# Routing slots computed per token, finer vector pieces between the score maxima, and a rearranged GpSimd queue in a one-core attention and tree feed-forward kernel

## The chip, the cores and the metric

The kernel runs on one core of a Trainium2 chip. The metric is device time in microseconds (us) for one launch. The engines are PE (TensorE: matmuls, transposes and, shown apart as PEld, weight loads), DVE (VectorE), ACT (ScalarE), POOL (GpSimd) and SP (SyncE, which here only issues DMAs). Each has its own instruction queue, worked in order, and waits on semaphores.

## What is computed

The input is 4 batches of 750 tokens with 128 features. In order:

```python
y = conv(sign(x), sign(kernel), taps=3)            # 4 x 748 x 64
h = (y + bias - moving_mean) * rsqrt(moving_var + 1e-3) + beta
qkv = layernorm(h) @ Wqkv + bqkv                   # 8 heads of 64
score = q . k * 64 ** -0.5 ; attn = softmax(score, axis=1)
av = attn[n, n] * v[n]                             # only the diagonal is used
h = h + av.reshape(b, n, 512) @ W0 + b0
x2 = layernorm(h) ; node = 0
for level in range(8):                             # a binary tree of 255 nodes
    score = x2 . w1s[node] + b1s[node]
    out += gelu(|score|) * (x2 @ w2s[node] + b2s[node])
    node = 2 * node + 1 + (score > 0)
h = h + out
```

## The kernel before

**Opening.** SP loads x. DVE makes signs, PE transposes them and runs the convolution, DVE turns it into h (`center`: scale, shift, two sums, difference, square) in four groups of six tiles, POOL computes the power -0.5 (`rstd1`), DVE multiplies (`normalise`), ACT and POOL split the result into two fp16 halves (`x_hi`, `x_lo`), and PE transposes it (fill "xh"). Group 0 serves the first projections. Before the loop DVE also centres groups 1 and 2; group 3 follows inside unit 0.

**Loop.** 16 units u (4 batches of 4 head pairs), each of 12 steps i (2 heads, 6 tiles of 125 tokens). A step is one score block of 125x748: PE `scores` (L914, four matmuls), DVE `maxima` (L1354), ACT `exps` (L1183). Three PSUM tiles rotate, so PE may be at most three steps ahead of ACT. The softmax denominator comes from the exps; the diagonal scores come from an elementwise product of q and k (POOL `qk_prod`) summed by PE (fill "d", L797), then `diag_shift` and `diag_weights` on DVE with `diag_exp` on ACT.

**Fills.** A hand-written table, `fills(u, i)`, says which smaller PE job follows the scores of a step: projections of q and k for unit u+2, value times W0 ("yt", or "yp" for the last batch), the convolution and transposes of the remaining groups, and the routing jobs of the batch before. All fills share the two halves of one PSUM tile in turn, and each is taken out of it by ACT one step earlier in ACT's order or by DVE one step later in DVE's. Other work is placed by (u, i) in the loops of DVE and ACT, and by u in POOL's loop. b is u//4 - 1, the batch whose attention is finished, and ph is u % 4. POOL's work per unit is `qk_lo` (low halves and product for unit u+2), `add_heads`, the second layer norm (`ln2_squares`, `ln2_rstd`, `ln2_x`; DVE does its reductions `ln2_sums` and `ln2_sumsq`), and `own_slots`: six indirect DMAs that scatter a batch's token rows into the table `sorted_rows` in HBM.

**Routing.** For batch b: transposes "t", node logits "L", `right_turns`, leaf match "A", `leaf_of_token` (mT: a 0/1 matrix, leaf by token), `leaf_counts` (a running count Ct along the tokens, then small column arithmetic), group prefix "pf", `group_slots`, then `slot_terms`: six DVE operations over 128x750 that turn the rank of each token into its slot, fp32 matmuls "sl" (L899) that sum over leaves, and `slots`. The last two batches' routing follows the last score, in the 4 pseudo-units after unit 15.

**Leaf stage.** SP loads sorted rows, PE multiplies them with the tree's matrices, ACT makes the gates, DVE weighs and sums, POOL scatters the output. It needs all rows scattered, and the low levels' table `wlow`, whose lower half POOL zeroes (L705) after the last score before SP puts the bias rows in.

## Time and profile before

| | us |
|---|---|
| median of 3 runs (563.11 to 563.93) | 563.47 |
| the profiled execution | 557.76 |
| its span | 555.8 |
| PE busy | 385.2 (69%) |
| DVE busy | 377.9 (68%) |
| ACT busy | 287.9 (52%) |
| POOL busy | 280.2 (50%) |

The page names no engine that is busy all the time. Its groups show 192 exps at 862 ns, 192 maxima at 931 ns and 768 score matmuls; before the exps ACT was idle for 95.3 us, nearly all of it released by a maximum, and before the maxima DVE was idle for 44.2 us. A busy share of the whole span therefore says little here: the reader looks at the stages (opening to 46 us, units 0 to 15 to 358.5 us, end of the routing to 424 us, leaf stage to 555.8 us) and within them at which engine was waiting and for whom. The stage table, and the timeline of a few stretches, are the views for that.

### The profile page before, as it was taken

Reading aid. Unit: us, or ns where it says so; the run is one execution under the profiler, and the core shown is the slowest. Engines: PE = TensorE matmul, PEld = TensorE weight load, DVE = VectorE, ACT = ScalarE, POOL = GpSimd, SP = SyncE. Lnnn points to the kernel's source line nnn. Section 1 sums busy time; section 2 is a strip of 40 time slices with the busy share of each in tenths; the row PEclk is TensorE's granted clock in tenths of the full one; section 3 lists DMA queues with packets and bytes.
Section 4 is the critical chain, followed back from the end, with each engine's and each line's share of the span. In section 5 each row is a group of like instructions: output and inputs, shape, how many; then the busy total and the mean of one; then the engine's idle time right before and its main releaser. Section 6 shows DMA issues by size and latency. Waiting matters only on the chain.

```text
span 555.8 us, 8129 instructions
## 1 busy us (share of the span) xinstructions
PE 385.2 (69%) x2554; PEld 261.6 (47%) x2554; DVE 377.9 (68%) x599; ACT 287.9 (52%) x688; POOL 280.2 (50%) x355
## 2 busy tenths in 40 slices
PE   0358589888958887839977788842304988787781
PEld 0245466555535544526644565520303766554450
DVE  1588766888855888997888956479601999842432
ACT  1346687998865876738957535300001333254551
POOL 5253748378894475674886331467181555512211
PEclk9977988999986998968998957555556999999996
DMA  5242423469498331230333000096014111000000
GB/s 121 70 108 60 108 59 84 112 150 199 108 158 141 84 83 27 57 83 19 95 83 84 1 2 0 16 133 70 3 45 128 31 52 49 9 6 7 6 2 6
DMA packets 58423, 36.98 MB, mean 67 GB/s; under 512 B 31645, under 2 KB 57079, under 8 KB 58378
## 3 DMA queue, kind: packets, MB, share of 16 engines
q1 hardware_dynamic: 54250, 33.55, 29.4%
q0 software_dynamic: 3328, 2.36, 1.7%
q10 hardware_dynamic: 800, 0.49, 0.4%
q8 instruction: 26, 0.43, 0.3%
q14 instruction: 19, 0.16, 0.1%
HBM read 11.15 MB, written 7.50 MB: 34 GB/s over the span
## 4 chain that ended last, share of the span: by engine, by line
DVE 34%; PE 27%; ACT 15%; issue 10%; POOL 8%; DMA 3%; DVEq 1%; POOLq 0%; ACTq 0%
PE Z L914 9%; ACT Z L1183 8%; DVE nm L1354 7%; DVE pre L1595 6%; PE Z L1051 4%; DVE va L1587 3%; DMA pre<-in_x 2%; ACT q L1125 2%; PE Z L1053 2%; POOL sorted_rows L649 2%; ACT k L1125 2%; POOL va L617 2%; PE Z L797 2%; DVE pre L320 2%; PE Z L1057 1%
## 5 line engine op out<-in xcount | busy, mean ns | idle before, releaser
L1183 ACT ACTIVATE Z<-Z,nm 125x748 f32<-125x748 f32 x192 | 165.4, 862 | 95.3 <-DVE nm L1354 94.4
L1354 DVE TENSOR_REDUCE nm<-Z 125x1 f32<-125x748 f32 x192 | 174.4, 931 | 44.2 <-PE Z L914 38.1
L914 PE MATMUL Z<-pool_a 128*125 128x512 f16 (+1 forms) x768 | 177.0, 361 | 36.8 <-ACT Z L1183 33.3
L914 PEld LDWEIGHTS Z<-pool_a 128*125 128x125 f16 x768 | 94.9, 150 | 85.8 <-ACT Z L1183 55.8
L721 POOL DMA_INDIRECT out<-pre,va x44 | 42.7, 971 | 87.3 <-DVE pre L1601 78.6
L1595 DVE TENSOR_REDUCE pre<-va 128x64 f32<-128x512 f32 x44 | 45.2, 1027 | 1.3
L1267 ACT COPY va<-Z 32x520 f32<-32x520 f32 x48 | 27.8, 580 | 30.0 <-PE Z L1057 26.6
L649 POOL DMA_INDIRECT sorted_rows<-xrow,slot x24 | 29.1, 1210 | 22.9 <-DVE slot L1488 15.4
L785 PE MATMUL Z<-xhT,wq 128*128 128x249 f16 (+1 forms) x192 | 34.5, 303 | 8.4 <-DVEq L1364 6.7
L1051 PE MATMUL Z<-pool_a,qk 128*32 x96 | 29.6, 390 | 14.2 <-ACT va L1267 8.8
L1183 ACT ACTIVATION_READ_ACCUMULATOR Z<-Z,nm 125x1 f32 x192 | 39.3, 205 | 0.0
L1587 DVE TENSOR_TENSOR va<-Z,gw 128x512 f32<-128x512 f32 x32 | 21.7, 679 | 24.3 <-ACT gw L1248 24.3
L591 POOL CAST pool_a<-q 128x748 f16<-128x748 f32 x14 | 11.3, 806 | 50.7 <-ACT q L1125 49.8
L1587 DVE TENSOR_TENSOR va<-va,gw 128x512 f32<-128x512 f32 x12 | 8.3, 692 | 38.3 <-ACT gw L1248 38.3
L617 POOL TENSOR_TENSOR va<-va 125x256 f32<-125x256 f32 (+2 forms) x54 | 29.6, 548 | 8.4 <-DVE va L1383 5.5
L797 PEld LDWEIGHTS Z<-sel,qk 128*125 128x125 f32 x192 | 28.5, 215 | 5.3 <-issue 1.6
L1239 ACT COPY qk<-Z 65x512 f32<-65x512 f32 x11 | 6.4, 581 | 45.0 <-PE Z L995 44.8
L601 POOL TENSOR_TENSOR qk<-q,k 128x748 f32<-128x748 f32 x16 | 29.4, 1838 | 0.0
L785 PEld LDWEIGHTS Z<-xhT,wq 128*128 128x128 f16 x192 | 19.7, 109 | 19.4 <-DVEq L1364 10.5
L797 PE MATMUL Z<-sel,qk 128*125 128x2 f32 x192 | 27.4, 248 | 0.4 <-DVE pre L1430 0.4
L593 POOL TENSOR_TENSOR pool_a<-q,pool_a 128x748 f16<-128x748 f32 x15 | 24.3, 1617 | 4.0 <-DVE pool_a L1309 2.9
L1016 PE MATMUL Z<-pool_a,qk 128*128 128x260 f32 x64 | 22.4, 433 | 4.4 <-DVE va L1587 4.1
(229 smaller groups left out, 653.8 us busy)
## 6 DMA issues: line engine op xcount, KB each, us to landing
pool_a<-pool_a SPq DMA_DIRECT2D x64, 187.0 KB, 3.3
pool_a<-pool_a SPq DMA_DIRECT2D x64, 93.5 KB, 2.2
sorted_rows<-zrow SPq DMA_DIRECT2D x1, 3640.0 KB, 21.1
va<-sorted_rows SPq DMA_DIRECT2D x11, 260.0 KB, 3.6
w<-in_L_ffn_w2s SPq DMA_DIRECT2D x1, 2048.0 KB, 16.9
pre<-in_x SPq DMA_DIRECT2D x4, 375.0 KB
pool_a<-in_L_ffn_w2s SPq DMA_DIRECT2D x1, 1024.0 KB
out<-pre,va POOLq DMA_INDIRECT x44
```

The lines of the kernel that those rows point to most:

```text
L601: gp.tensor_tensor(qk[:, w % 3, 0:N], q32[:, w % 2, 0:N], k32[:, w % 2, 0:N], ALU.mult).then_inc(s_prod, 1)
L617: link(gp.tensor_tensor(pw[:, 0:n], pw[:, 0:n], pw[:, n:2 * n], ALU.add))
L649: gp.indirect_dma_start(rows, bass.IndirectOffsetOnAxis(slots[0:XP, t:t + 1].bitcast(u32), 0), xrow[0:XP, t, :], None, bounds_check=SLOTS - 1,
L721: gp.indirect_dma_start(outf, bass.IndirectOffsetOnAxis(ids.bitcast(u32), 0), yo[:, k % NO, :], None, bounds_check=T - 1, oob_is_err=False ...
L785: last = mm(z[:, PSUM_AT[c] % 512:PSUM_AT[c] % 512 + CLASS_N[c]], wq[:, a, g * H * D + j * P:g * H * D + (j + 1) * P], xhT[:, r0:r0 + CLAS ...
L797: last = mm(z[0:XP, t:t + NT + 1:NT], qk[:, w % 3, KST[t]:KST[t] + XP], sel[:], start=True, stop=True)
L914: last = mm(z[0:XP, c0:c1], kst[:, u % 3, a, hd, KST[t]:KST[t] + XP], qst[:, u % 3, hd, c0:c1], start=(a == 0), stop=(a == 1))
L1051: mm(y[:, 0:4 * E1], xg, wlow[:, bass.ds(node(g, 4) * (4 * E1) + T03 * E1, 4 * E1)], start=True, stop=True)
L1183: sc_.activation(z, z, ACT.Exp, bias=nm[0:XP, u % 4, i:i + 1], accum_out=sm[0:XP, u % 4, i:i + 1]).then_inc(s_exp, 1)
L1354: v.tensor_reduce(nm[0:XP, u % 4, i:i + 1], Z[n % 3][0:XP, 0:N], X, ALU.max, negate=True).then_inc(s_max, 1)
L1587: v.tensor_tensor(wy[:, k % 2].rearrange("p (h l o) -> p h l o", h=2, o=D), y[:, :, :, 0:D], gw[:, k % 4].rearrange("p (h l) -> p h l", h= ...
L1595: v.tensor_reduce(yo[:, k % NO, :], wy[:, k % 2].rearrange("p (l o) -> p o l", o=D), X, ALU.add).then_inc(s_sl, 1)
```

## The change

- **Opening.** PE computes the batch-norm rows before the first transposes, and ACT copies them first. Only group 0 is centred before the loop. `center` takes a piece number: six pieces, for group 1 in unit 0, group 2 in unit 2, group 3 in unit 3, each behind one of the maxima of steps 0 to 5 (for groups 2 and 3 the first piece is the taking of the fill). `normalise` moves to (0,8), (3,1) and (4,1), and POOL's `rstd1` and `x_lo` with it; SP's writes and reads of h move one or two units back.
- **Second layer norm.** `ln2_sums` moves from step 4 to step 9 of ph 2, `ln2_sumsq` from there to step 1 of ph 3, `ln2_rstd` and `ln2_x` to the head of POOL's ph 3. `path_matrix` moves from unit 4 to 2 on POOL, `h_bias` of batches 2 and 3 from unit 3 to 7.
- **Diagonal.** `diag_weights` runs at step 7 instead of 5, but still at 5 in the pseudo-unit after the last.
- **Routing.** `leaf_counts` is cut into `leaf_ranks` (step 1), `leaf_counts` (3) and `rank_of_token` (5). `slot_terms` is gone: only the token's own rank, Ct times mT, in fp16, is made over 128x750; the per-leaf terms become six columns, split into two fp16 parts, and PE sums both over the leaves with 18 fp16 matmuls instead of 6 fp32 ones; `slots` does the comparisons per token (five small operations). mT, Ct and Xt are fp16.
- **Last units.** The fills of units 14 and 15 are placed anew; batch 2's leaf match starts in unit 15, its slots are ready before batch 3's transposes, and POOL scatters batch 2 before it writes the low columns of the table. ACT writes the table's zeros (three copies) instead of POOL.

```diff
-GROUPS_FOR = {"q": (1, 2, 2, 2), "k": (1, 2, 3, 3), "v": (3, 4, 4, 4)}
+GROUPS_FOR = {"q": (1, 2, 2, 2), "k": (1, 2, 3, 3), "v": (4, 4, 4, 4)}
...
-Ct, Xt, T1, T2 = [pre[:, NIN * n:NIN * (n + 1)] for n in range(4)]
...
-mT = pre[:, 3072 + TH:3072 + 2 * TH].bitcast(bf16)
+mT, Ct, Xt = [pre[:, 3072 + TH * n:3072 + TH * (n + 1)].bitcast(f16) for n in (1, 2, 3)]
...
-FIRST = [("xb", 2), ("xb", 3), ("cv", 2)]
+FIRST = [("xb", 2), ("xb", 3), ("cv", 1)]
...
-    f += {(0, 1): [("xh", 1)], (0, 2): [("wt", 0)], (0, 7): [("wm", 0)], (0, 8): [("xh", 2)], (0, 9): [("cv", 3)],
-          (0, 11): [("wt", 1)], (1, 7): [("wm", 1)], (1, 8): [("xh", 3)], (1, 9): [("wt", 2)],
-          (1, 11): [("wm", 2)], (2, 7): [("cb", 0)], (2, 9): [("w1", 0)]}.get((u, i), [])
+    f += {(0, 2): [("wt", 0)], (0, 8): [("wm", 0)], (0, 10): [("wt", 1)], (1, 1): [("xh", 1)],
+          (1, 8): [("wm", 1)], (1, 10): [("wt", 2)], (1, 11): [("cv", 2)], (2, 8): [("wm", 2)], (2, 9): [("cb", 0)],
+          (2, 11): [("cv", 3)], (3, 8): [("xh", 2)], (3, 10): [("w1", 0)], (4, 6): [("xh", 3)]}.get((u, i), [])
...
-    if u == NU - 2 and i in (7, 8, 10, 11):
-        f.append(("yp", LASTB + i // 10, (0, 1)[i in (8, 11)]))
-    if u == NU - 1 and i in (7, 9):
-        f.append(("yp", u - 1, (i - 7) // 2))
+    if u == NU - 2:
+        f += {4: [("yp", LASTB, 0)], 6: [("yp", LASTB, 1)], 8: [("yp", LASTB + 1, 0)],
+              10: [("yp", LASTB + 1, 1)]}.get(i, [])
+    if u == NU - 1:
+        f += {5: [("t", b, 0)], 6: [("t", b, 1)], 7: [("L", b, 0)], 8: [("L", b, 1)], 9: [("yp", u - 1, 0)],
+              10: [("A", b, 0)], 11: [("yp", u - 1, 1)]}.get(i, [])
...
-    if 0 <= b < B - 1 and ph == 3:
+    if 0 <= b < B - 2 and ph == 3:
         f += {7: [("t", b, 0)], 8: [("t", b, 1)], 9: [("L", b, 0)], 10: [("L", b, 1)]}.get(i, [])
...
-        f += {(0, 3): [("A", b - 1, 0)], (0, 4): [("A", b - 1, 1)], (0, 5): [("yp", NU - 1, 0)],
-              (0, 6): [("yp", NU - 1, 1)], (0, 9): [("pf", b - 1)], (1, 0): [("t", b, 0)], (1, 1): [("t", b, 1)],
+        f += {(0, 0): [("A", b - 1, 1)], (0, 5): [("yp", NU - 1, 0)], (0, 6): [("yp", NU - 1, 1)],
+              (0, 8): [("pf", b - 1)], (0, 10): [("sl", b - 1)], (1, 0): [("t", b, 0)], (1, 1): [("t", b, 1)],
               (1, 2): [("L", b, 0)], (1, 3): [("L", b, 1)], (1, 5): [("A", b, 0)], (1, 6): [("A", b, 1)],
-              (2, 0): [("pf", b)], (2, 1): [("sl", b - 1)], (2, 2): [("sl", b)]}.get((ph, i), [])
+              (2, 0): [("pf", b)], (2, 2): [("sl", b)]}.get((ph, i), [])
...
+CENTERED = {0: 1, 2: 2, 3: 3}
+NORMED = {(0, 8): 1, (3, 1): 2, (4, 1): 3}
...
-def slot_terms(b, eng, ops, link):
...
-    link(ops.tensor_scalar(T1, Ct, float(G + 1), col[:, c_d0], ALU.is_ge, ALU.mult))
-    link(ops.tensor_scalar(T2, Ct, col[:, c_cap], col[:, c_d1], ALU.is_ge, ALU.mult))
-    link(ops.tensor_tensor(T1, T1, T2, ALU.add))
-    link(ops.tensor_scalar(T1, T1, col[:, c_jm], 1.0, ALU.add, ALU.mult))
-    link(ops.tensor_tensor(T1, T1, Ct, ALU.add))
-    ops.tensor_tensor(Xt, T1, mT, ALU.mult).then_inc(s_xt, 1)
...
-    rstd1(2)
-    x_lo(2)
...
+    rstd1(1)
     for u in range(NU + NPAIR):
         b, ph = u // NPAIR - 1, u % NPAIR
-        if u == 1:
-            rstd1(3)
-            x_lo(3)
+        if u in (3, 4):
+            x_lo(u - 1)
+        if 0 <= b < B - 1 and ph == 3:
+            ln2_rstd(b)
+            ln2_x(b)
         if u + AHEAD < NU:
             qk_lo(u + AHEAD)
+        if u == 0:
+            x_lo(1)
         if u == 1:
             token_numbers()
+        if u == 2:
+            rstd1(2)
+            path_matrix()
         if u == 3:
+            rstd1(3)
             h_bias(0)
             h_bias(1)
+        if u == 4:
+            leaf_columns()
+        if u == 7:
             h_bias(2)
             h_bias(3)
         if 0 <= b < B - 1 and ph < 2:
             for t in range(3 * ph, 3 * ph + 3):
                 add_heads(b, t)
+        if u == NU - 2:
+            add_pair(LASTB)
         if 0 <= b < B - 1 and ph == 2:
             ln2_squares(b)
-            ln2_rstd(b)
-            ln2_x(b)
-        if u == NU - 2:
-            add_pair(LASTB)
+        if b >= 1 and ph == 3 and b < B - 1:
+            own_slots(b - 1)
         if NU - 2 <= u < NU:
             add_pair(u - 1)
-        if u == 4:
-            path_matrix()
-            leaf_columns()
-        if b >= 1 and ph == 3 and b < B - 1:
-            own_slots(b - 1)
         if u == NU:
             ln2_rstd(B - 1)
             pool.sem_inc(s_rs2, 1)
-    pool.wait_ge(s_score, 2 * NT * NU)
-    link(gp.memset(wlow[D:P, :], 0.0))
-    pool.sem_inc(s_zl, 1)
-    pool.wait_ge(*full(("d", NU - 1)))
-    link(gp.memset(xsT[D:P], 0.0))
-    pool.sem_inc(s_zl, 1)
+    own_slots(B - 2)
+    pool.wait_ge(s_zl, LOWZ)
     low_columns()
-    own_slots(B - 2)
     own_slots(B - 1)
...
-    x_blocks(0, Z[0]).then_inc(s_xtp, 1)
-    x_blocks(1, Z[0][:, 512:1024]).then_inc(s_xtp, 1)
-    pe.wait_ge(s_kq, 1)
-    conv(0, Z[1]).then_inc(s_cv, 1)
     pe.wait_ge(s_bnp, 1)
...
     last.then_inc(s_bnb, 1)
-    conv(1, Z[1][:, 512:1024]).then_inc(s_cv, 1)
+    x_blocks(0, Z[0]).then_inc(s_xtp, 1)
+    x_blocks(1, Z[0][:, 512:1024]).then_inc(s_xtp, 1)
+    conv(0, Z[1]).then_inc(s_cv, 1)
...
     def slots(b):
         z = take(("sl", b))
         pe.wait_ge(s_xt, b + 1)
+        pe.wait_ge(s_vn, b + 1)
         for t in range(NT):
-            last = mm(z[0:XP, t:t + 1], Xt[:, t * HALF:(t + 1) * HALF], onef[:], start=True, stop=True)
+            zt, ts = z[0:XP, 6 * t:6 * t + 6], slice(t * HALF, (t + 1) * HALF)
+            for n in range(2):
+                mm(zt, mT[:, ts], leaf16[:, n], start=(n == 0), stop=False)
+            last = mm(zt[:, 0:2], Xt[:, ts], one16[:], start=False, stop=True)
         last.then_inc(s_full, 1)
...
+        act.wait_ge(s_score, 2 * NT * NU)
+        m = LOWN * E1 // LOWZ
+        for n in range(LOWZ):
+            sc_.copy(wlow[D:P, n * m:(n + 1) * m], zrow[D:P, 0:1].to_broadcast([D, m])).then_inc(s_zl, 1)
+        sc_.copy(xsT[D:P].rearrange("p r c -> p (r c)"), zrow[D:P, 0:1].to_broadcast([D, 1536])).then_inc(s_zl, 1)
...
+    act.wait_ge(s_bnb, 1)
+    sc_.copy(bn[:].rearrange("p a d -> p (a d)"), Z[3][:, 512:512 + 2 * D]).then_inc(s_bn, 1)
     act.wait_ge(s_xtp, 1)
     x_copy(0, Z[0]).then_inc(s_xtc, 1)
     act.dma_start(wst[0:D, :], Wqkv).then_inc(s_w, 16)
...
-    act.wait_ge(s_bnb, 1)
-    sc_.copy(bn[:].rearrange("p a d -> p (a d)"), Z[3][:, 512:512 + 2 * D]).then_inc(s_bn, 1)
...
-    x_hi(1)
...
-            if (u, i) in ((0, 7), (1, 7), (1, 11)):
-                vw0_hi(u + i // 11)
-            if (u, i) in ((0, 4), (1, 4)):
-                x_hi(2 + u)
-            if (u, i) == (2, 9):
+            if u < 3 and i == 8:
+                vw0_hi(u)
+            if (u, i - 1) in NORMED:
+                x_hi(NORMED[u, i - 1])
+            if (u, i) == (3, 3):
                 v_bias_low()
             if 1 <= u <= NU and i == 4:
                 diag_exp(u - 1)
-    act.wait_ge(s_zl, 2)
+            if (u, i) == (NU, 4):
+                table_zeros()
...
+    def center(b, n, z):
...
+        if n == 0:
+            dve.wait_ge(*(full(("cv", b)) if b else (s_cv, 1)))
+            if b == 0:
...
+            v.tensor_tensor(hv, hv, bn[:, 1:2, :].to_broadcast([P, NT, D]), ALU.add).then_inc(s_hn, 1)
+            dve.wait_ge(s_hn, b + 1)
+        elif n == 2:
+            link(v.tensor_reduce(l[:, 0, :], hv, X, ALU.add))
+            link(v.tensor_scalar(l[:, 0, :], l[:, 0, :], -1.0 / D, None, ALU.mult))
+        elif n == 3:
+            link(v.tensor_tensor(c, hv, l[:, 0, :].unsqueeze(2).to_broadcast([P, NT, D]), ALU.add))
+        elif n == 4:
+            link(v.tensor_tensor(sq[:], c, c, ALU.mult))
+        else:
+            link(v.tensor_reduce(l[:, 1, :], sq[:], X, ALU.add))
+            v.tensor_scalar(l[:, 2, :], l[:, 1, :], 1.0 / D, LN_EPS, ALU.mult, ALU.add).then_inc(s_sum, 1)
...
-    center(0, Z[1])
+    for n in range(6):
+        center(0, n, Z[1])
...
-    center(1, Z[1][:, 512:1024])
...
-    normalise(1)
...
-    center(2, zone(("cv", 2)))
...
-    def leaf_counts(b):
...
-        link(v.tensor_tensor_scan(Ct, ones[:, 0:1].to_broadcast([P, NIN]), mT, col[:, c_cnt], ALU.mult, ALU.add))
-        last = Ct[:, NIN - 1:NIN]
...
+        link(v.tensor_tensor_scan(Ct, ones[:, 0:1].to_broadcast([P, NIN]), mT, zrow[:, 0:1], ALU.mult, ALU.add))
...
+        link(v.tensor_tensor(col[:, c_new0], col[:, c_cnt], Ct[:, NIN - 1:NIN], ALU.add))
+        link(v.tensor_scalar(ogi[:, 0:1], col[:, c_new0], -1.0, float(G - 1), ALU.add, ALU.max))
...
-        v.tensor_copy(col[:, c_cnt], last)
...
+    def rank_of_token(b):
+        v.tensor_tensor(Xt, Ct, mT, ALU.mult).then_inc(s_xt, 1)
+        v.tensor_scalar(col[:, c_cap], col[:, c_grp], float(G), float(G + 1), ALU.mult, ALU.add)
...
+        v.tensor_tensor(leaf[:, 4:5], col[:, c_last], col[:, c_j32], ALU.subtract)
...
+        if b:
+            dve.wait_ge(*full(("sl", b - 1)))
+        link(v.tensor_copy(leaf16[:, 0, :], leaf[:]))
+        v.tensor_tensor(leaf16[:, 1, :], leaf[:], leaf16[:, 0, :], ALU.subtract).then_inc(s_vn, 1)
+        dve.wait_ge(s_vn, b + 1)
...
-        v.tensor_tensor(slf[0:XP], zone(("sl", b))[0:XP, 0:NT], dup_out[0:XP], ALU.add).then_inc(s_fd, 1)
+        z = zone(("sl", b))[0:XP, 0:6 * NT].rearrange("p (t c) -> p t c", c=6)
+        e = beyond[0:XP, :, 0:2]
+        link(v.tensor_copy(slf[0:XP], z[:, :, 0]))
+        link(v.tensor_tensor(e, slf[0:XP].unsqueeze(2).to_broadcast([XP, NT, 2]), z[:, :, 2:4], ALU.is_ge))
+        link(v.tensor_tensor(e, e, z[:, :, 4:6], ALU.mult))
+        link(v.tensor_reduce(slf[0:XP], beyond[0:XP], X, ALU.add))
+        v.tensor_tensor(slf[0:XP], slf[0:XP], z[:, :, 1], ALU.add).then_inc(s_fd, 1)
         dve.wait_ge(*freed["sl", b])
...
+            if u == 0 and i == 0:
+                center(1, 0, zone(("cv", 1)))
             for f in dve_takes(u, i):
                 take(f)
-            if (u, i) in ((0, 2), (1, 3)):
-                normalise(2 + u)
-            if (u, i) == (2, 9):
+            if u in CENTERED and 1 <= i < 6:
+                center(CENTERED[u], i, None)
+            if (u, i) in NORMED:
+                normalise(NORMED[u, i])
+            if (u, i) == (3, 2):
                 dve.wait_ge(s_ch, 1)
                 v.tensor_tensor(c32[:, 1, :], c32[:, 0, :], cb[0:3, :], ALU.subtract).then_inc(s_cl, 1)
-            if 1 <= u <= NU and i == 5:
+            if 1 <= u <= NU and i == (7 if u < NU else 5):
                 diag_weights(u - 1)
-            if 1 <= b < B - 1 and ph == 2 and i == 6:
-                slot_terms(b - 1, dve, v, link)
-            if u == NU and i == 11:
-                slot_terms(B - 2, dve, v, link)
-            if 0 <= b < B - 1 and ph == 2 and i == 4:
+            if 0 <= b < B - 1 and (ph, i) == (2, 9):
                 ln2_sums(b)
-            if 0 <= b < B - 1 and ph == 2 and i == 9:
+            if 0 <= b < B - 1 and (ph, i) == (3, 1):
                 ln2_sumsq(b)
-            if 1 <= b < B - 1 and ph == 1 and i == 1:
+            if 1 <= b < B - 1 and (ph, i) == (1, 1):
+                leaf_ranks(b - 1)
+            if 1 <= b < B - 1 and (ph, i) == (1, 3):
                 leaf_counts(b - 1)
+            if 1 <= b < B - 1 and (ph, i) == (1, 5):
+                rank_of_token(b - 1)
+            if (u, i) == (NU, 3):
+                leaf_ranks(B - 2)
+            if (u, i) == (NU, 4):
+                leaf_counts(B - 2)
             if u == NU and i == 8:
                 last_heads(NU - 1)
                 ln2_sums(B - 1)
                 ln2_last()
-                leaf_counts(B - 2)
+                rank_of_token(B - 2)
+            if u == NU and i == 9:
                 ln2_last_x()
             if u == NU + 1 and i == 8:
+                leaf_ranks(B - 1)
                 leaf_counts(B - 1)
-            if u == NU + 2 and i == 1:
-                slot_terms(B - 1, dve, v, link)
+                rank_of_token(B - 1)
```

## Rows read from the trace of the kernel before

**Rows 1.** Two groups of the page (count, busy, mean ns, idle before).

```profile
L1183 ACT ACTIVATE Z<-Z,nm 125x748 f32<-125x748 f32 x192 | 165.4, 862 | 95.3 <-DVE nm L1354 94.4
...
L785 PEld LDWEIGHTS Z<-xhT,wq 128*128 128x128 f16 x192 | 19.7, 109 | 19.4 <-DVEq L1364 10.5
```

**Rows 2.** Windows by stage, cut at first maxima of units; the first line names the columns.

```profile
core 0: us, PE busy (x) PEld busy (x) DVE busy (x) ACT busy (x) POOL busy (x), PEclk, DMA share, GB/s
0.00:46.00 46.00, 17.89 (x135) 13.40 (x135) 25.64 (x44) 14.05 (x25) 20.16 (x50) 0.89 0.43 108
46.00:89.40 43.40, 33.64 (x228) 24.41 (x226) 29.13 (x41) 33.67 (x78) 23.63 (x41) 0.88 0.32 75
89.40:150.40 61.00, 53.09 (x328) 34.20 (x328) 51.21 (x67) 53.70 (x127) 41.83 (x59) 1.00 0.64 129
150.40:190.40 40.00, 29.54 (x152) 19.47 (x150) 25.84 (x37) 27.44 (x65) 27.25 (x32) 0.83 0.83 136
190.40:229.10 38.70, 31.41 (x181) 19.97 (x181) 32.38 (x58) 27.48 (x64) 23.38 (x30) 0.96 0.26 65
229.10:254.20 25.10, 15.40 (x78) 10.63 (x77) 22.00 (x28) 12.35 (x30) 14.54 (x15) 0.73 0.19 47
254.20:269.40 15.20, 13.78 (x88) 9.50 (x88) 12.71 (x18) 14.23 (x34) 8.09 (x7) 1.00 0.27 64
307.10:358.50 51.40, 41.64 (x194) 29.21 (x195) 33.02 (x50) 23.83 (x52) 13.15 (x18) 0.75 0.00 1
358.50:424.00 65.50, 16.78 (x72) 11.50 (x72) 35.82 (x78) 2.69 (x6) 36.33 (x28) 0.50 0.43 67
424.00:555.80 131.80, 101.29 (x940) 70.19 (x940) 78.32 (x132) 51.22 (x147) 42.71 (x44) 0.95 0.10 26
```

**Rows 3.** Timeline of the opening: start, us, engine, line, what [idle before <-releaser].

```profile
17.94 0.56 DVE L1295 TENSOR_TENSOR pre<-Z,bn 128x384 f32<-128x384 f32 x1 [4.41 <-ACT bn L1202]
...
41.19 2.73 PE L914 MATMUL Z<-pool_a 128*125 128x512 f16 x8 [2.65 <-DMA pool_a<-pool_a]
...
45.99 2.62 DVE L1354 TENSOR_REDUCE nm<-Z 125x1 f32<-125x748 f32 x3
```

**Rows 4.** Timeline of POOL in unit 1.

```profile
86.78 7.03 POOL L533 MEMSET w<- 64x8320 f32 x1
```

**Rows 5.** Timeline of DVE in unit 6.

```profile
161.20 0.55 DVE L1516 TENSOR_REDUCE ln<-xrow 128x6 f32<-128x384 f32 x1 [5.26 <-POOL xrow L618]
...
170.38 0.55 DVE L1520 TENSOR_REDUCE ln<-sq 128x6 f32<-128x384 f32 x1 [2.37 <-POOL sq L636]
```

**Rows 6.** Timeline of DVE in unit 10.

```profile
238.93 0.83 DVE L320 TENSOR_SCALAR pre<-pre,col 128x750 f32<-128x750 f32 x1
...
246.21 1.44 DVE L325 TENSOR_TENSOR pre<-pre 128x750 f32<-128x750 f32 x1
```

**Rows 7.** Timeline of PE in units 14 and 15.

```profile
317.70 0.85 PE L914 MATMUL Z<-pool_a 128*125 128x512 f16 x4
322.38 2.68 PE L899 MATMUL Z<-onef,pre 128*125 128x1 f32 x12 [3.84 <-DVEq L1403]
...
335.58 1.49 PE L914 MATMUL Z<-pool_a 128*125 128x512 f16 x4
```

**Rows 8.** Timeline from the last score to the first matmul of the leaf stage.

```profile
371.90 8.87 POOL L705 MEMSET pool_a<- 64x10530 f32 x1 [0.15 <-POOL ln L641]
...
374.26 6.92 DVE L320 TENSOR_SCALAR pre<-pre,col 128x750 f32<-128x750 f32 x1
...
401.06 1.30 POOL L649 DMA_INDIRECT sorted_rows<-xrow,slot  x1 [15.37 <-DVE slot L1488]
...
402.68 0.16 DVE L1486 TENSOR_TENSOR slf<-Z,dup_out 125x6 f32<-125x6 f32 x1 [2.55 <-PE Z L899]
...
417.61 1.19 POOL L649 DMA_INDIRECT sorted_rows<-xrow,slot  x1 [0.30 <-issue]
...
423.98 1.09 PE L995 MATMUL Z<-idf,va 128*65 128x128 f32 x4 [20.82 <-DMA va<-sorted_rows]
```

83 lines of the change are left out of this document (39 added, 44 removed).

## The prediction

> **What bounds the kernel now.** I read four views in this order. The page's groups say that ACT's exps make up 165 us and that ACT stood idle for 95 us before them, behind maxima [rows 1]. The stage table [rows 2] says where: units run in 15 to 15.5 us when nothing disturbs them (unit 11 is 254.2 to 269.4, and all of PE, ACT and DVE are near 13 to 14 us busy in it), but units 0 and 1 take 43.4 together, 6 and 7 take 40.0, unit 10 takes 25.1, and 14 and 15 take 51.4. Then 65.5 us pass between the last score and the leaf stage with ACT busy for 2.7 of them. The timelines name the causes: DVE, which works its queue in order, stands 5.3 us for POOL's head sums and 2.4 us for POOL's squares in unit 6 [rows 5]; `slot_terms` holds DVE from 238.9 to 247.7, so no maximum is taken and PE and ACT stop [rows 6]; PE then gives 2.7 us to the fp32 slot matmuls; and after such a pause the granted clock is at 1.2 GHz, where a score block takes 1.49 instead of 0.85 us [rows 7]; the PEclk column is 0.73 to 0.88 in just these units [rows 2]. At the end the path is: DVE's `slot_terms` of batch 2, of which the first operation alone takes 6.9 us beside POOL's 8.9 us memset, all routing of batch 3 behind it, then twelve scatters one after another, since batch 2's slots wait for batch 3's [rows 8].
>
> **The change, part by part, on the profiled execution (557.8 us, span 555.8; the median of the timed runs is 5.7 higher, and I carry that distance over).**
>
> Opening. The batch-norm matmuls leave the path between convolution and `center`: -1.4 (PE's 1.1 and ACT's copy of 0.3, which end at the start of the first row of [rows 3]). Group 1's centering, six operations of 0.56 and two small ones, 3.9 us in all, no longer stands ahead of DVE's split of the first k; ACT's output of k, itself 1.4 earlier, then sets it, so the split is ready about 2.9 earlier. The first scores follow its DMAs as now: 41.2 becomes 38.3 [rows 3]. They then waited until 46.0 for a maximum because DVE was centering group 2, beside POOL; that is gone, so the first maximum comes at about 39.5: **-6.5**. ACT's Wqkv load is issued some 3.5 us later, behind the first transposes; ACT's first cast of it now starts only after the conversion of x, with some 3 us of DVE work between it and its reader, so I count nothing, and up to +2 if it lands late.
>
> Units 0 and 1 lose a 4 us block (group 3), two transposes with their copies, and one w0 product; they gain group 1's six pieces. DVE has 12 maxima of 0.87 per unit [rows 3], ACT 12 exps of 0.86 [rows 1] and, by my estimate from unit 11's 14.2 us of ACT, some 3 of projections. With the pieces, w0 products and copies I add up 16 us for either engine in unit 0; an undisturbed unit is some 10 to 20% longer than its busiest engine, so I take 19.5, and 17.5 in unit 1: 37.0 against 43.4 [rows 2], **-6.4**.
>
> Units 2 and 3 pay: each gets a centering (3.7 us) and its share of w0 and transposes. Steps 2 to 5 carry ACT's projections, and half a us of DVE per step is hidden there; steps 0 and 1 hide nothing. In unit 2 POOL's 7.0 us memset, 18.7 us into unit 1 now [rows 4] and about 15 with less ahead of it, reaches 3 to 4 us into unit 2, and the second piece reads two tensors from SBUF. A DVE operation that takes 0.8 elsewhere [rows 6] lasted 6.9 beside such a memset [rows 8]; I take 2 us for it (bounds 0 and 4). They took 30.4 of the 61.0 us of units 2 to 5; I take 38.4: **+8.0**. Unit 4 gets a `normalise` and the last transposes: **+1.6**.
>
> This is where the Trainium skill speaks against the change: its GPSIMD Engine Reference (Specifications) says that GpSimd shares its SBUF interface with VectorE and that the two contend when a DVE instruction has two SBUF inputs or runs in a 2-port mode. By that rule, the 6.9 us in [rows 8] agree, also each later two-input piece would meet POOL's low halves and products, and the sum would be that of the first rival below.
>
> Unit 6 and 7. `ln2_sums` five steps later finds POOL's head sums done, the more so as the 9 us of `path_matrix` have left unit 4. -4.6 of the 5.3, since a step costs 1 anyway. `ln2_sumsq` moves to (7,1); POOL has then done `qk_lo` of unit 8, about 14 us into unit 6, and the squares, 16 us, while DVE is there after 17: no wait, but only 1 us of slack. With the slow clock after the stalls gone, 32.1 against 40.0: **-7.9**.
>
> Units 8 and 9, and 12 and 13: the same scan, cut in three. The rank step adds an fp16 product over 750 columns (0.4 to 0.9 us) and some six column operations of 0.16 [rows 8]; cutting the 3.3 us block hides part of it: **+0.7** for each pair.
>
> Unit 10. Without `slot_terms` -8.7 from the step [rows 6]. PE's fp32 sum of 2.7 [rows 7] becomes 18 fp16 matmuls; their weight loads, for which the nearest row is 109 ns for 128 columns [rows 1], make it 2.0, bounded by nothing but issue (0.5) and by the fp32 price per matmul, 0.22, times 18 (4.0). `slots` grows by 1 us, `ln2_sums` is in step 9. 17.1 against 25.1: **-8.0**. Unit 11 gets the reduction: **+0.6**.
>
> Units 14 and 15. The 8.8 us of `slot_terms` and the slow clock behind them go. PE was busy for 41.6 of the 51.4 us [rows 2]; nine of its score blocks stood at the slow clock, 0.64 us each too long [rows 7], and the slot matmuls shrink by 1.4 (at full clock I take 1.3 for them), so 34.5 remain. Unit 11 is 10% longer than its PE work [rows 2]; with value products, a leaf match and their round trips through ACT and DVE I take 20%: 41.4 against 51.4, **-10.0**.
>
> The end, from the last maximum (357.6, T). The diagonals now wait for the last value product and for DVE: +2.8. DVE: shift at T+4.2, scan and counts to T+7.5, weights, last heads and layer norm to T+13 (now T+11), rank, group slots (POOL's power under them), T+17.1, `ln2_last_x` T+17.7 (now T+15). PE sums batch 2's slots before batch 3's transposes, +2 at the slow clock; transposes, logits and leaf match as timed now, mT at T+25.6, then scan 2.0, counts 1.1, rank 1.9, group slots 2.4, PE 2.0, `slots` 1.2: batch 3's slots at T+35.9, against 403.0 = T+45.5 [rows 8]. Batch 2's slots are there at T+20.2; POOL's six scatters, 1.5 us apart, run T+21 to T+30, the low columns to T+33, batch 3's six from T+36.8, the last at T+44.2. It landed and was loaded 6.4 us after its start [rows 8]: T+50.6, against 424.0 = T+66.4: **-15.9**. The zeros cost nothing: 12,066 columns of ACT at the price of an exp (748 in 0.86) are 13.9 us, from T+4.6 to T+18.5, before the transposes' copies at T+19.5. If that cover is gone, each us late is a us of the end. The leaf stage, 131.8, is untouched.
>
> Sum: -6.5 -6.4 +8.0 +1.6 -7.9 +0.7 +0.7 -8.0 +0.6 -10.0 -15.9 = -43.1. Profiled execution 514.7; median **520.4 us**.
>
> **The rivals.**
> - *POOL's interface holds the pieces* (0.17). Nine two-input pieces each wait about 1 us behind POOL's operations of 1.6 to 1.8, and the memset holds the one in unit 2 for 4. For it: [rows 8]. Against: POOL is idle in steps 0 to 3 of a disturbed unit. +9: 529.
> - *The waits move with POOL* (0.13). `ln2_sumsq` is ahead of the squares after all, 3 to 4 us each in units 7 and 11, and the slow clock follows as it does now [rows 5]. +9: 529.
> - *The slots aren't cheaper* (0.06): if 18 matmuls cost 4.0 us and `slots` and the rank step 2 us more than taken, each of four batches gives back some 4: +16, 536. That is the case of a change that doesn't do what it says.
> - *Slower than before* (0.03): the denser PE is granted 1.2 GHz in the loop. A score costs 0.64 more [rows 7]; it decides from 68 further scores of 192 at that level, since 68 x 0.64 is 43. With 80 more it is 520.4 + 51 = 572. Against: units 2 to 5 are PE's busiest stretch, 87%, and have a granted clock of 1.00 [rows 2].
>
> **How the numbers follow.** The forecast has 0.61. Its own bounds are -9 (pieces fully hidden, units 14 and 15 at 38, slot matmuls at 0.5 us) and +6. The first two rivals lie at 529 with the same spread; so 511 to 535 leaves out the third, the fourth and some of the edges, under 0.2. A measurement of this kernel tells apart about 0.2%, 1.1 us. Faster 0.95, same 0.01, slower 0.04.
>
> **What would show it.** First maximum near 39.5. No DVE wait on POOL in units 6 and 7. Unit 10 near 17 us and PEclk at 1.00 in it. Two-input pieces of `center` at 0.56 us; one of 2 to 4 us in unit 2. The last scatter's start at about 44 us after the last maximum and 6 scatters before the low columns. Wrong it would be made by a step in which DVE or ACT waits for a semaphore that POOL sets late, above all at (7,1), (3,1) and (4,1), or by ACT still writing zeros when batch 3's transposes are ready.

## The result and the profile after

After the change the kernel takes 497.4 us (median of four runs, 493.7 to 506.6), before it 563.3; the ratio is 0.882, with an interval of 0.876 to 0.888. The forecast was 520.4 us, with 511 to 535 as its range: the direction was right, and the time fell by 66 us where 43 had been worked out. Executions of one kernel differ with the clock that TensorE was granted: the four of after are 493.7, 497.1 and 497.6 us at a mean clock of 0.913 to 0.917, and 506.6 at 0.889, and with the six of the run without an edit below the ten span 2.6%, while one execution of before (0.56) and one of an edited kernel (0.60) took 644 and 592 us and count in no ratio.

The stages of the profiled execution (497.1 us, span 495.4), each cut at the first maximum of a unit as in [rows 2]. The first window is the opening, then units 0 and 1, 2 and 3, 4 and 5, 6 and 7, 8 and 9, unit 10, unit 11, units 14 and 15, the end up to the leaf stage, the leaf stage:

```profile
core 0: us, PE busy (x) PEld busy (x) DVE busy (x) ACT busy (x) POOL busy (x), PEclk, DMA share, GB/s
0.00:39.40 39.40, 12.95 (x99) 9.69 (x100) 14.37 (x27) 13.72 (x24) 16.08 (x49) 0.93 0.45 111
39.40:73.90 34.50, 30.95 (x215) 21.61 (x214) 28.05 (x39) 30.09 (x71) 21.51 (x40) 0.93 0.41 99
73.90:111.40 37.50, 26.99 (x204) 19.27 (x203) 34.62 (x49) 30.18 (x70) 30.63 (x39) 1.00 0.30 70
111.40:144.10 32.70, 28.73 (x172) 18.23 (x172) 27.46 (x38) 27.57 (x67) 22.37 (x29) 1.00 1.01 188
144.10:173.20 29.10, 25.22 (x151) 16.23 (x149) 24.82 (x37) 26.99 (x65) 22.56 (x27) 1.00 1.05 166
173.20:211.40 38.20, 31.68 (x182) 19.91 (x183) 33.80 (x66) 27.41 (x64) 23.65 (x31) 0.96 0.28 69
211.40:227.00 15.60, 12.40 (x90) 8.69 (x90) 13.23 (x24) 12.21 (x29) 10.09 (x12) 1.00 0.25 62
227.00:242.80 15.80, 14.41 (x82) 10.08 (x81) 12.64 (x20) 14.04 (x34) 10.23 (x10) 0.89 0.27 67
280.40:315.30 34.90, 30.65 (x189) 21.12 (x188) 29.00 (x47) 22.46 (x50) 16.98 (x20) 0.95 0.05 12
315.30:363.30 48.00, 15.89 (x93) 11.40 (x93) 23.68 (x90) 14.03 (x10) 20.39 (x23) 0.52 0.57 84
363.30:495.40 132.10, 102.01 (x940) 70.52 (x940) 78.35 (x132) 51.15 (x147) 42.70 (x44) 0.95 0.10 26
```

The forecast of each stage against this, in us (units 14 and 15 up to the last maximum, where before took 50.5 and the forecast therefore had 40.5):

| stage | before | forecast | after | after less forecast |
|---|---|---|---|---|
| opening | 46.0 | 39.5 | 39.4 | -0.1 |
| units 0, 1 | 43.4 | 37.0 | 34.5 | -2.5 |
| units 2, 3 | 30.4 | 38.4 | 37.5 | -0.9 |
| units 4, 5 | 30.6 | 32.2 | 32.7 | +0.5 |
| units 6, 7 | 40.0 | 32.1 | 29.1 | -3.0 |
| units 8, 9 | 38.7 | 39.4 | 38.2 | -1.2 |
| unit 10 | 25.1 | 17.1 | 15.6 | -1.5 |
| units 12, 13 | 37.7 | 38.4 | 37.6 | -0.8 |
| units 14, 15 | 50.5 | 40.5 | 34.9 | -5.6 |
| end | 66.4 | 50.6 | 48.0 | -2.6 |
| unit 11, leaf stage | 147.0 | 147.6 | 147.9 | +0.3 |

These add up to -17.4 in the span. The other 5.5 us of the miss are the distance from the profiled execution to the median, carried over as 5.7 us; here it was 0.2. So no part went the wrong way: many small terms came out better than taken, and one by 5.6.

The page's groups say what the loop gained. ACT's idle time before the exps was 95.3 us [rows 1]:

```profile
L1183 ACT ACTIVATE Z<-Z,nm 125x748 f32<-125x748 f32 x192 | 166.1, 870 | 61.5 <-DVE nm L1367 61.2
```

The exps last as long as before (870 against 862 ns); the 34 us come out of waits for maxima. The PEclk column, 0.73 to 0.83 in the windows of units 6 and 7, unit 10, and units 14 and 15 of [rows 2], is 0.95 to 1.00 in the same units here.

The waits of [rows 5] are gone. DVE's two reductions of the layer norm, now at (6,9) and (7,1), with POOL's squares between them:

```profile
156.06 0.54 DVE L1547 TENSOR_REDUCE ln<-xrow 128x6 f32<-128x384 f32 x1
...
158.97 0.83 POOL L633 TENSOR_TENSOR sq<-cent 128x384 f32<-128x384 f32 x1
...
160.24 0.54 DVE L1551 TENSOR_REDUCE ln<-sq 128x6 f32<-128x384 f32 x1
```

Neither has idle time ahead of it, but the second starts 0.4 us after the squares end (159.8): the slack is smaller than the 1 us of the forecast.

The end, which was [rows 8]: ACT's zeros, the slot matmuls of batch 2, the first and the last scatter of each batch, and the leaf stage's first matmul.

```profile
318.69 9.05 ACT L1196 COPY pool_a<-zrow 64x5265 f32<-64x5265 f32 x2
...
327.65 1.46 ACT L1197 COPY qk<-zrow 64x1536 f32<-64x1536 f32 x1
...
330.31 0.35 PE L898 MATMUL Z<-leaf,pre 128*125 128x6 f16 x2 [6.89 <-DVE leaf L1502]
...
332.12 0.24 PE L899 MATMUL Z<-one,pre 128*125 128x2 f16 x1
332.40 0.16 DVE L1513 COPY slf<-Z 125x6 f32<-125x6 f32 x1 [1.20 <-PE Z L899]
...
334.51 1.29 POOL L646 DMA_INDIRECT sorted_rows<-xrow,slot  x1 [5.06 <-DVE slot L1519]
...
343.42 1.19 POOL L646 DMA_INDIRECT sorted_rows<-xrow,slot  x1 [0.30 <-issue]
...
349.38 1.21 POOL L646 DMA_INDIRECT sorted_rows<-xrow,slot  x1 [3.67 <-DVE slot L1519]
...
356.86 1.19 POOL L646 DMA_INDIRECT sorted_rows<-xrow,slot  x1 [0.30 <-issue]
363.31 1.08 PE L995 MATMUL Z<-idf,va 128*65 128x128 f32 x4 [14.72 <-DMA va<-sorted_rows]
```

From the last maximum (T, 315.3) the steps came at T+15.0 (batch 2's matmuls), T+19.2 to T+29.3 (its scatters), T+34.1 to T+41.6 (batch 3's), and the leaf stage 6.45 us behind the start of the last. The forecast had T+21 to T+30, T+36.8 to T+44.2 and 6.4 us.

### The profile page after: what moved, and what is told of

It reads as the page before. It is cut to its first block, busy times and chain, and to the rows that moved or that the text cites. A ratio compares the mean times of both kernels' runs of the same rounds, so it can differ in the third digit from the quotient of the medians.

```text
span 495.4 us, 8210 instructions
## 1 busy us (share of the span) xinstructions
PE 362.6 (73%) x2578; PEld 246.1 (50%) x2578; DVE 353.8 (71%) x619; ACT 297.0 (60%) x691; POOL 266.6 (54%) x354
## 4 chain that ended last, share of the span: by engine, by line
DVE 39%; PE 27%; ACT 15%; issue 11%; DMA 5%; POOL 1%; SPq 1%; DVEq 0%; POOLq 0%; ACTq 0%
DVE nm L1367 12%; ACT Z L1183 8%; PE Z L914 8%; DVE pre L1634 6%; PE Z L1051 5%; DVE va L1626 4%; DMA pre<-in_x 3%; DVE va L1396 2%; PE Z L1053 2%; ACT q L1125 2%; PE Z L1057 2%; DVE pre L1463 1%; ACT k L1125 1%; ACT va L1276 1%; PE Z L1055 1%
## 5 line engine op out<-in xcount | busy, mean ns | idle before, releaser
L1367 DVE TENSOR_REDUCE nm<-Z 125x1 f32<-125x748 f32 x192 | 175.4, 932 | 38.9 <-PE Z L914 33.2
L914 PE MATMUL Z<-pool_a 128*125 128x512 f16 (+1 forms) x768 | 164.5, 342 | 27.3 <-ACT Z L1183 23.7
L914 PEld LDWEIGHTS Z<-pool_a 128*125 128x125 f16 x768 | 88.7, 141 | 71.6 <-ACT Z L1183 45.6
L781 PE MATMUL Z<-xhT,wq 128*128 128x249 f16 (+1 forms) x192 | 33.4, 295 | 10.5 <-DVEq L1377 9.2
L1183 ACT ACTIVATION_READ_ACCUMULATOR Z<-Z,nm 125x1 f32 x192 | 41.1, 214 | 0.0
L1051 PE MATMUL Z<-pool_a,qk 128*32 x96 | 29.6, 390 | 14.1 <-ACT va L1276 8.7
L646 POOL DMA_INDIRECT sorted_rows<-xrow,slot x24 | 30.4, 1266 | 15.3 <-DVE slot L1519 8.7
L1626 DVE TENSOR_TENSOR va<-Z,gw 128x512 f32<-128x512 f32 x32 | 21.7, 679 | 18.6 <-ACT gw L1257 18.4
L781 PEld LDWEIGHTS Z<-xhT,wq 128*128 128x128 f16 x192 | 19.2, 106 | 21.1 <-DVEq L1377 13.4
L588 POOL CAST pool_a<-q 128x748 f16<-128x748 f32 x14 | 11.3, 806 | 32.2 <-ACT q L1125 32.2
L793 PEld LDWEIGHTS Z<-sel,qk 128*125 128x125 f32 x192 | 25.4, 194 | 6.0 <-DVEq L1416 1.1
L598 POOL TENSOR_TENSOR qk<-q,k 128x748 f32<-128x748 f32 x16 | 28.3, 1772 | 0.0
L1255 ACT ACTIVATE gw<-Z 128x8 f32<-128x8 f32 x32 | 5.7, 177 | 35.3 <-PE Z L1023 33.7
L793 PE MATMUL Z<-sel,qk 128*125 128x2 f32 x192 | 25.2, 236 | 1.4 <-DVEq L1416 0.9
## 6 DMA issues: line engine op xcount, KB each, us to landing
sorted_rows<-zrow SPq DMA_DIRECT2D x1, 3640.0 KB, 22.1
w<-in_L_ffn_w2s SPq DMA_DIRECT2D x1, 2048.0 KB, 16.6
```

What stands on the lines that cost most here:

```text
L646: gp.indirect_dma_start(rows, bass.IndirectOffsetOnAxis(slots[0:XP, t:t + 1].bitcast(u32), 0), xrow[0:XP, t, :], None, bounds_check=SLOTS - 1,
L781: last = mm(z[:, PSUM_AT[c] % 512:PSUM_AT[c] % 512 + CLASS_N[c]], wq[:, a, g * H * D + j * P:g * H * D + (j + 1) * P], xhT[:, r0:r0 + CLAS ...
L793: last = mm(z[0:XP, t:t + NT + 1:NT], qk[:, w % 3, KST[t]:KST[t] + XP], sel[:], start=True, stop=True)
L914: last = mm(z[0:XP, c0:c1], kst[:, u % 3, a, hd, KST[t]:KST[t] + XP], qst[:, u % 3, hd, c0:c1], start=(a == 0), stop=(a == 1))
L1051: mm(y[:, 0:4 * E1], xg, wlow[:, bass.ds(node(g, 4) * (4 * E1) + T03 * E1, 4 * E1)], start=True, stop=True)
L1183: sc_.activation(z, z, ACT.Exp, bias=nm[0:XP, u % 4, i:i + 1], accum_out=sm[0:XP, u % 4, i:i + 1]).then_inc(s_exp, 1)
```

## The experiments

"Trace" is the profiled execution of each kernel. Medians of this kernel move by several us, so small effects are read from the trace, unit by unit, and larger ones from both. A trace is one execution too. In the three others whose edits lie elsewhere or that have none (centering as one block, zeros by POOL, no edit), units 14 and 15 took 33.7 to 36.1 us and unit 10 16.6 to 17.6, where after's trace has 34.9 and 15.6; units 6 and 7 took 29.1 in all of them. Each diff shows the part of the edit that matters; "..." marks what is left out.

**Slot terms over the whole row put back.** After, with `slot_terms` and its call sites, fp32 slot matmuls against a column of ones, and the old count columns:

```diff
-                    for n in range(2):
-                        mm(zt, mT[:, ts], leaf16[:, n], start=(n == 0), stop=False)
-                    last = mm(zt[:, 0:2], Xt[:, ts], one16[:], start=False, stop=True)
+                    last = mm(z[0:XP, t:t + 1], Xt[:, t * HALF:(t + 1) * HALF], onef[:], start=True, stop=True)
...
+                    if 1 <= b < B - 1 and (ph, i) == (2, 6):
+                        slot_terms(b - 1, dve, v, link)
```

> The changed kernel with slot_terms and the fp32 slot matmuls put back, all else kept. Both theories: +8.5 us in unit 10, the same in unit 14, two times 4.9 at the end less 3 for the small operations saved there. Theory A (the forecast left out that after a pause all of PE's work runs at 1.2 GHz, not the score blocks alone): units 14 and 15 take 47 to 50 us instead of 34.9, and their PE busy time rises from 30.7 to 36 or more; total +29 to +34, so about 528. Theory R (only the vector operations themselves count, the clock is incidental): units 14 and 15 take 43 to 44, PE busy there rises by the 1.4 us of the slot matmuls, total +23.

Measured: 517.1 us against 559.6 for before on that chip, ratio 0.925 (0.917 to 0.934), so 20 us above after. In the trace unit 10 is 23.5 us (+7.9), the end 56.7 (+8.7), units 14 and 15 39.9 (+5.0). Both theories had more, in these two units and in total (+23, and +29 to +34). PE was busy there for 33.2 us, where the first theory wanted 36 or more and the second 32.1, so this run decides for neither. The price of the terms was right in unit 10 and at the end; of the 15.6 us that units 14 and 15 gained they explain a third alone. Units 9 and 13, whose rank step here lacks the product `Xt` and some column operations, came out 1.6 us shorter each; the forecast had 0.7 as the price of the new rank step. [rows 6] answer to this run's DVE in unit 10, the first and the last of six:

```profile
218.48 1.53 DVE L329 TENSOR_SCALAR pre<-pre,col 128x750 f32<-128x750 f32 x1
...
226.52 0.94 DVE L334 TENSOR_TENSOR pre<-pre 128x750 f32<-128x750 f32 x1
```

**The order in which unit 15's products, transposes, logits and leaf match are issued.** All of them at steps 7 to 11, instead of one at each of steps 5 to 11:

```diff
-                f += {5: [("t", b, 0)], 6: [("t", b, 1)], 7: [("L", b, 0)], 8: [("L", b, 1)], 9: [("yp", u - 1, 0)],
-                      10: [("A", b, 0)], 11: [("yp", u - 1, 1)]}.get(i, [])
+                f += {7: [("yp", u - 1, 0), ("t", b, 0)], 8: [("t", b, 1)], 9: [("yp", u - 1, 1), ("L", b, 0)],
+                      10: [("L", b, 1)], 11: [("A", b, 0)]}.get(i, [])
```

> The changed kernel with unit 15's fills late again: value products at steps 7 and 9, transposes at 7 and 8, node logits at 9 and 10, first leaf match at 11. Theory A (the chain transposes, copy, logits, comparison, match has its round trips in the last five steps and PE waits in order at each): unit 15 goes from 15.3 to 21 to 24, and the end gets no longer; total +5 to +8. Theory R (it was the slow clock of the kernel before that made unit 15 long): +1 to +2.

Measured: 506.4 us, ratio 0.899 (0.892 to 0.907); unit 15 is 21.2 instead of 15.3. PE in that unit: it waits twice for DVE to free a bank, and the score block behind the second wait takes 1.45 instead of 0.80 (the kernel before has the same two waits, 1.68 and 1.41):

```profile
311.26 0.80 PE L914 MATMUL Z<-pool_a 128*125 128x512 f16 x4
313.74 0.54 PE L862 MATMUL Z<-idf,xrow 125*65 125x125 f32 x3 [1.68 <-DVEq L1416]
...
319.61 1.62 PE L876 MATMUL Z<-xT,w1T 65*128 65x375 f32 x2 [1.42 <-DVEq L1416]
321.02 1.45 PE L914 MATMUL Z<-pool_a 128*125 128x512 f16 x4
```

The waits themselves are 3.1 us and the unit is 5.9 longer. PE spent 7.5 us of the unit at 1.2 GHz, none in after's trace; work at half speed in that time can make up the rest.

**Unit 14's products.** Before's places for them, steps 7, 8, 10 and 11, in after:

```diff
-                f += {4: [("yp", LASTB, 0)], 6: [("yp", LASTB, 1)], 8: [("yp", LASTB + 1, 0)],
-                      10: [("yp", LASTB + 1, 1)]}.get(i, [])
+            if u == NU - 2 and i in (7, 8, 10, 11):
+                f.append(("yp", LASTB + i // 10, (0, 1)[i in (8, 11)]))
```

> The changed kernel with unit 14's four value products at steps 7, 8, 10 and 11 again instead of 4, 6, 8 and 10. With slot_terms put back, units 14 and 15 took 39.9 us, not the 50.5 of the kernel before, so 10.6 us must lie in how the fills are placed. Theory A (the placing in both units): unit 14 goes from 19.6 to 23 or more, since products of 1.8 us on PE follow each other within three steps and then PE's work outruns the three score tiles; total +3 to +5. Theory R (only the routing fills of unit 15 and the slow clock matter): 0 to +1.

Measured: 498.9 us (495.2 to 505.1), ratio 0.888 (0.878 to 0.898), units 14 and 15 34.0 instead of 34.9. Equal code differs by more than that (33.7 to 36.1), so no difference that the runs can tell.

**Terms and both fill orders together.** The three edits above in one kernel:

> After with three things put back together that were run one by one before: slot_terms with fp32 slot matmuls (units 14 and 15 39.9, +5.0), unit 14's products at steps 7, 8, 10, 11 (-0.9 for both units) and unit 15's transposes, logits and leaf match late (+2.5 for both units in the trace). Additive theory (three independent prices): 34.9 + 5.0 - 0.9 + 2.5 = 41.5, against 50.5 in the trace of before. Compound theory (each makes a gap, and the slow clock behind a gap lengthens the next one): 45 to 49 for units 14 and 15, with over 20 us of them at 1.2 GHz. Unit 10 and the end as in the run with slot_terms alone: 23.5 and T+56.7.

Measured: 529.2 us, ratio 0.944 (0.938 to 0.949). Units 14 and 15 take 52.6 us, longer than the upper end of the compound theory and than before's 50.5:

```profile
286.50:313.20 26.70, 21.16 (x100) 15.22 (x99) 18.97 (x28) 11.59 (x25) 5.77 (x10) 0.70 0.00 1
313.20:339.10 25.90, 21.75 (x86) 14.29 (x84) 13.80 (x21) 11.39 (x25) 13.36 (x13) 0.63 0.06 15
```

The additive sum as it was written took 2.5 for unit 15's fills, where the trace had shown 5.9; with 5.9 it is 44.9, still 7.7 short. Unit 10 came out as expected (23.5), the end at T+57.9 where 56.7 was expected. The view that explains the gap is PEclk. At 1.2 GHz the column counts half, so the time at that level is twice (1 - PEclk) times the window: 35 us of 52.6 here, 25 of 50.5 before [rows 2], 3.5 of 34.9 in after, and in the runs with one edit alone

```profile
286.00:309.80 23.80, 18.80 (x101) 13.80 (x100) 19.55 (x30) 10.94 (x24) 5.77 (x11) 0.81 0.00 1
309.80:325.90 16.10, 14.40 (x84) 9.68 (x83) 13.28 (x20) 11.61 (x28) 11.42 (x11) 0.96 0.11 26
```

(the terms) 9 + 1 us, and

```profile
282.70:302.30 19.60, 19.20 (x120) 14.15 (x118) 15.80 (x28) 10.96 (x24) 5.58 (x10) 0.85 0.00 1
302.30:323.40 21.10, 15.82 (x73) 9.30 (x73) 13.10 (x20) 11.65 (x27) 13.26 (x13) 0.82 0.08 19
```

(the fills) 6 + 8 us. Each alone leaves most of the two units at 2.4 GHz; together they leave a third of them. PE's busy time shows the price: 30.65 us in after, 33.2 and 35.0 with one edit, 42.9 with all, for the same scores and products and some slot matmuls (1.7 us of the difference); 12.3 of the 17.7 us are that. The 7.7 us are more than traces of equal code differ by in these units (2.4); no run has two of the edits alone, so which pair makes them is open. Undoing three parts of the change brings this stage back to where it was before.

**The layer norm's reductions at their old places, (2,4) and (2,9).**

```diff
-                    if 0 <= b < B - 1 and (ph, i) == (2, 9):
+                    if 0 <= b < B - 1 and (ph, i) == (2, 4):
                         ln2_sums(b)
-                    if 0 <= b < B - 1 and (ph, i) == (3, 1):
+                    if 0 <= b < B - 1 and (ph, i) == (2, 9):
                         ln2_sumsq(b)
```

(and POOL's steps behind them one unit earlier)

> The changed kernel with the second layer norm's reductions at steps 4 and 9 of ph 2 again and POOL's part in one piece, but path_matrix left in unit 2. Theory A (each place of the reduction decides): batch 0's head sums are done at 148.4, DVE comes to step 4 at 149.3, so no wait there; POOL's squares end at 159.8 and DVE comes to step 9 at 156, so a wait of about 4 us in units 6 and 10 each: +6 to +8. Theory R (the 9 us of path_matrix in unit 4 were the whole cause): no wait, 0.

Measured: 508.5 us, ratio 0.907 (0.900 to 0.915). Units 6 and 7 take 35.2 instead of 29.1, unit 10 19.0 instead of 15.6. DVE waits for the squares in unit 6:

```profile
149.69 0.54 DVE L1546 TENSOR_REDUCE ln<-xrow 128x6 f32<-128x384 f32 x1
...
160.05 0.55 DVE L1550 TENSOR_REDUCE ln<-sq 128x6 f32<-128x384 f32 x1 [3.69 <-POOL sq L633]
```

The head sums are no longer late; the run with both undone, below, shows that their wait came from `path_matrix`. The wait is the 4 us of the first theory, but the kernel is 11 us slower where 6 to 8 were expected.

**`path_matrix` in unit 4 instead of unit 2.** The call moves from `if u == 2` to `if u == 4`.

> The changed kernel with path_matrix in unit 4 again, the reductions late as in the change. Theory A: POOL runs some 7 us later in units 5 and 6, head sums at 155.5 just before step 9 (156.0), but the squares only near 165 while DVE is at step 1 of unit 7 at 160: a wait of 4 to 5 us, total +4 to +5. Theory R (late reductions alone are enough): 0 to +1.

Measured: 505.9 us (497.9 to 506.7, too scattered for a ratio; the shortest is no longer than after's, so what this costs in total is not shown). In the trace unit 7 is 19.4 instead of 15.0; unit 6 stays at 14.1. The wait moved one unit on:

```profile
157.07 0.54 DVE L1547 TENSOR_REDUCE ln<-xrow 128x6 f32<-128x384 f32 x1
...
164.59 0.55 DVE L1551 TENSOR_REDUCE ln<-sq 128x6 f32<-128x384 f32 x1 [3.25 <-POOL sq L633]
```

**Both together.**

> Both undone together. Waits in unit 6 as before the change, 5 us at step 4 and 2 to 4 at step 9, and 4 at step 9 of unit 10. With the slow clock behind them +11 to +14; if the two were one cause, no more than the larger of the other two runs.

Measured: 512.3 us, ratio 0.916 (0.907 to 0.924), 15 us above after. Unit 6 is 22.1 us again, as long as before, and its waits are nearly those of [rows 5]:

```profile
154.21 0.55 DVE L1546 TENSOR_REDUCE ln<-xrow 128x6 f32<-128x384 f32 x1 [5.25 <-POOL xrow L615]
...
163.40 0.55 DVE L1550 TENSOR_REDUCE ln<-sq 128x6 f32<-128x384 f32 x1 [3.00 <-POOL sq L633]
```

So both halves are needed: the earlier `path_matrix` takes away the first wait, the later reductions the second.

**Table zeros by POOL in after.** `table_zeros` is taken from ACT, and POOL's two memsets stand ahead of `own_slots(B - 2)` again.

> The changed kernel with the table's zeros written by POOL again, after the last rstd and ahead of batch 2's scatters. Queue theory: POOL writes from 14 to 24.6 us after the last maximum, batch 2's scatters start at 24.6 instead of 19.2, low columns end at 38, batch 3's scatters start there instead of 34.1: +4. Interface theory: the memset also holds the next DVE operation that reads one fp32 tensor of more than one column in a two-port mode, the copy of the leaf terms into fp16 (128x6, 0.17 us now), until the memset ends: that copy takes 8 us or more, everything of batch 3 behind it: +8.5. Two-input operations beside the memset keep their 0.56 in either theory, as one did in unit 2 of the changed kernel.

Measured: 506.5 us, ratio 0.900 (0.894 to 0.907). The end is 56.4 us instead of 48.0 (+8.4). A cast of 128 by 6 elements, 0.17 us in after, ends when the memset ends:

```profile
331.73 8.87 POOL L706 MEMSET pool_a<- 64x10530 f32 x1 [0.15 <-POOL ln L638]
331.73 0.15 DVE L1501 TENSOR_TENSOR leaf<-col 128x1 f32<-128x1 f32 x1
331.92 8.71 DVE L1504 CAST leaf<-leaf 128x6 f16<-128x6 f32 x1
```

**Table zeros by ACT in the kernel before.** That part of the change alone:

```diff
-            pool.wait_ge(s_score, 2 * NT * NU)
-            link(gp.memset(wlow[D:P, :], 0.0))
+            pool.wait_ge(s_zl, 2)
...
+                    if (u, i) == (NU, 4):
+                        table_zeros()
```

> The kernel before, with one thing of the change alone: the zeros of wlow and xsT are written by ACT from a zero column after the last score instead of by POOL's two memsets. Interface theory (POOL's long fp32 memsets hold DVE's 2-port operations to their own end): the first operation of slot_terms for batch 2, 6.92 us beside the 8.87 us memset, falls to its usual 0.6 to 0.8 and the second from 1.69 to 0.68, so the end is 7 us shorter: about -7.3 against before. Queue theory (DVE was late for other reasons, and the memset only stood beside it): 0. If ACT's 10.6 us of zeros collide with its copies of the transposes, up to 3 of the gain are lost.

Measured: 551.7 us against 559.7, ratio 0.983 (0.978 to 0.989). The end is 59.2 us instead of 66.4, -7.2, and the first operation of [rows 8]'s `slot_terms` takes 0.61 instead of 6.92:

```profile
375.79 0.61 DVE L320 TENSOR_SCALAR pre<-pre,col 128x750 f32<-128x750 f32 x1
```

**The diagonal's weights at step 5 instead of 7.** `if 1 <= u <= NU and i == 5:`

> The changed kernel with diag_weights at step 5 of every unit. In the forecast this move had no price. Theory A: at step 5 DVE waits 1.3 us for ACT's exp of the diagonal, beside which ACT is the bound anyway, and in units 2 to 4 the move costs 1.4 us behind POOL's operation, which step 5 would not meet at full length: between -2 and +2. Theory R (the wait at step 5 is on the path in each of 14 units): step 5 goes from 1.21 to 1.9 us as in the kernel before, +0.7 per unit, +8 to +10.

Measured: 503.4 us, ratio 0.898 (0.892 to 0.904); in the trace the loop is 3.0 us longer (279.0). That lies between the two theories (at most 2, and 8 to 10). DVE now waits for ACT's exp of the diagonal, 1.60 us in units 5 and 6 alike; the row of unit 6:

```profile
153.24 0.79 DVE L1384 TENSOR_TENSOR at<-at,sm 125x12 f32<-125x12 f32 x1 [1.60 <-ACT at L1189]
```

Units 5 to 8 are 0.6 to 0.7 us longer for it; the other units differ both ways.

**Each centering as one block at step 1**, instead of a piece at each of steps 1 to 5 of units 0, 2 and 3:

```diff
-                    if u in CENTERED and 1 <= i < 6:
-                        center(CENTERED[u], i, None)
+                    if u in CENTERED and i == 1:
+                        for n in range(1, 6):
+                            center(CENTERED[u], n, None)
```

> After, with the five later pieces of each centering at step 1 of units 0, 2 and 3 as one block, instead of one at each of steps 1 to 5. If cutting the block is what makes it cheap (each piece hidden behind scores): DVE gives no maximum for 2.8 us, PE's three score banks fill, and each of the three units is 1.5 to 3 longer: +4 to +8 in all, with a stretch of 1.2 GHz. Rival (DVE is the busiest engine there, so the same work costs the same wherever it stands): 0 to +1.5.

Measured: 507.2 us, ratio 0.905 (0.900 to 0.911), against 499.3 for the unedited kernel in the same batch. Against that kernel's trace unit 0 is 2.1 us longer, unit 1 1.1, unit 2 3.0, unit 3 1.3, together 7.5: the first theory. In unit 2 the block runs into POOL's memset (76.54 to 83.57), as a piece does in the unedited kernel, where the same scaling took 2.42:

```profile
79.17 0.55 DVE L1308 TENSOR_TENSOR pre<-pre,bn 128x384 f32<-128x384 f32 x1
79.75 0.55 DVE L1311 TENSOR_REDUCE ln<-pre 128x6 f32<-128x384 f32 x1
80.33 3.26 DVE L1312 TENSOR_SCALAR ln<-ln 128x6 f32<-128x6 f32 x1
```

So 0.8 of the 7.5 us is the longer hold and not the block.

**Three places where DVE was held by POOL, moved at once:** unit 14's products as above, `Xt` at step 2, the diagonal's weights at step 5 in units 1 to 4.

```diff
+                    if 1 <= b < B - 1 and (ph, i) == (1, 2):
+                        v.tensor_tensor(Xt, Ct, mT, ALU.mult).then_inc(s_xt, 1)
...
-                    if 1 <= u <= NU and i == (7 if u < NU else 5):
+                    if 1 <= u <= NU and i == (7 if 4 < u < NU else 5):
```

> After with three small moves: unit 14's value products at steps 7, 8, 10, 11 (a run without other edits had unit 14 1.9 us shorter), Xt = Ct x mT at step 2 of units 9 and 13 instead of step 5 (it lasted 1.83 there beside POOL, 0.54 elsewhere), and diag_weights at step 5 in units 1 to 4 (1.4 to 1.6 us at step 7 there, 0.17 elsewhere). If waits at POOL's interface cost their full length: 1.9 + 2 x 1.3 + 3 x 1.3, up to -7, and -3 to -5 with what other engines hide. If DVE had that much slack at these steps: 0 to -2, all of it from unit 14. diag_weights at step 5 may instead wait for ACT's exps, as it did in later units: then +1 to +2.

Measured: 501.8 us (495.7 to 504.5), ratio 0.895 (0.891 to 0.900), so nothing gained. In the trace the holds did go (`Xt` 0.54 us instead of 1.83, the weights 0.17 in units 2 and 3; in unit 4 a wait of 1.98 for ACT took their place), and the loop was 275.2 us, 0.8 less than in after, which is no more than unit 14's products gave alone (275.1). A hold also came back: in units 9 and 13 the weights now took 1.41 us instead of 0.41 beside POOL, and these units were 0.5 us longer. So the run shows that these moves gain nothing, and not that a hold costs nothing.

**After with no edit**, in the same batch:

> After, with no edit, on the same chip as the three above and over five rounds: its times and granted clocks show how far equal kernels differ, and the others of this batch are compared with it. Expected: 497 within 4, ratio to before 0.88; the runs with the lower granted clock are the longer ones.

Measured: 499.3 us (495.8 to 506.7), ratio 0.887 (0.883 to 0.892). In its trace PE spent 34.9 us of the loop at 1.2 GHz, in after's 18.5, and the loop was 2.3 us longer. Two traces of one kernel differ by as much as several of the terms of the sum; no version tried is measurably faster than after.

## Why the prediction was right in direction and too small

The time is 13.6 us below the range. Of the 23.0 us between forecast and result, units 14 and 15 are 5.6, the distance from trace to median 5.5, and the other terms together 11.8, nearly all on one side; the forecast's own lower bound had 9 for all of them. The step that failed is the price of units 14 and 15: 34.5 us of PE work and 20% on top, where 30.65 and 14% were measured.

- *Opening.* First maximum at 39.35, forecast 39.5. Right; no run undoes its parts one by one.
- *Units 0 and 1.* The step "19.5 and 17.5" added up 16 us of work for unit 0 and put 22% on it, more than its own 10 to 20%. The work was right: DVE was busy for 15.96 us of unit 0. But the unit took 16.3, hardly more than its busiest engine; the margin was wrong. Unit 1 took 18.2.
- *Units 2 and 3.* +7.1 against +8.0, and +8.7 in the trace of after with no edit. The term for the memset (2 us, bounds 0 and 4) was put on the wrong operation. The memset ran from 72.07 to 79.10, the two-input piece in the middle of it took 0.55, and the tiny scaling of the sums was held to its end:

```profile
72.07 7.03 POOL L530 MEMSET w<- 64x8320 f32 x1
...
76.16 0.55 DVE L1308 TENSOR_TENSOR pre<-pre,bn 128x384 f32<-128x384 f32 x1
77.59 0.54 DVE L1311 TENSOR_REDUCE ln<-pre 128x6 f32<-128x384 f32 x1
78.17 0.96 DVE L1312 TENSOR_SCALAR ln<-ln 128x6 f32<-128x6 f32 x1
```

How long it is held depends on where the memset ends. In the trace of after with no edit it was 2.42 us, and unit 2 took 21.1 instead of 19.6:

```profile
77.52 2.42 DVE L1312 TENSOR_SCALAR ln<-ln 128x6 f32<-128x6 f32 x1
```

- *Units 6 and 7.* Mechanism right, as the three runs on it show (5.3 and 3 us of waits, both causes named); the size was -10.9 instead of -7.9. The forecast's 32.1 us left a margin over engines that then had a clock of 1.00 and no wait for POOL (ACT was busy for 27.0 of the 29.1 us).
- *Unit 10.* -9.5 against -8.0. The 18 slot matmuls were taken at 2.0 us. At full clock they took 1.16; at the end, at 1.2 GHz, 2.05 (330.31 to 332.36). The rest of the miss is not clear of noise, since unit 10 took 16.6 to 17.6 in other traces of the same code.
- *Units 14 and 15.* The step that failed. It took PE's busy time from 41.6 to 34.5 by taking 0.64 us off each of nine score blocks and 1.4 off the slot matmuls, and then put 20% on top. PE's busy time came out at 30.65, and the stage 14% above it. By kind of matmul, the score blocks gave back 4.4 us and not 5.8; the slot matmuls gave 1.7; and work that the forecast had left at its old length gave the rest. The four logit matmuls took 3.2 us before and 1.6 after, products and bias rows 0.9 less, and the diagonals 3.2 less, of which 1.9 are unit 15's, which in after run behind the last maximum. (Matmuls overlap a little, so the kinds add up to more than the total.) The kernel before spent 25 us of this stage at 1.2 GHz, with PE busy for 23.6 of them, and that stretched everything in it. The run with terms and fills together shows the same from the other side: 12.3 us of PE time and 17.7 us of stage return. And the forecast did not price the new order of the fills at all, which is worth 5.9 us alone and more with the terms.
- *The end.* 48.0 against 50.6, with each step 1 to 3 us early and the order of the steps as written: zeros hidden (they end at T+13.8, 4 us before the copies that they could have delayed), six scatters of batch 2 ahead of batch 3's, the last 6.45 us before the leaf stage. The run with POOL's memset put back costs 8.4, and ACT's zeros alone in before bring 7.2: of the 18.4 us of the end, the zeros' move is about 7 to 8 and the terms 8.7. The 1 to 3 us that are left, batch 2's scatters ahead of the low columns among them, were not tested by themselves.
- *The rivals.* The interface holds DVE more widely than the forecast's own case had it (the product `Xt` 1.83 instead of 0.54, the weights 1.43 to 1.56 instead of 0.17 in units 2 to 4, and the squares piece of `center` 0.98 and 1.05 in units 2 and 3 and the first `normalise` 1.82, instead of 0.56), but moving those of `Xt` and of the weights changed nothing that can be measured. The waits did not move with POOL, though with 0.4 us to spare. The slots were cheaper. The denser PE was not granted less: the loop spent 18.5 us at 1.2 GHz (34.9 in the second trace), and 69.5 before. Units 2 to 5, which the forecast calls PE's busiest stretch at 87%, are not quite that: unit 11 has 91%, at a clock of 1.00 too [rows 2].
- *The distance to the median.* 5.7 us were carried over as if they belonged to every kernel like this. They were the clock of particular runs: before's runs fall in two groups, 558 and 563 us, and the profiled one was of the lower. That is a quarter of the miss, and could have been seen from two times of before that differ by 1%. Three timings also gave the forecast its 0.2% for what a measurement tells apart, where executions of after differ by 2.6%.

## What to carry to other kernels

When a stage has a PEclk below 1, its gain is not the stall that is removed but the stall plus the slow time behind it. Take twice (1 - PEclk) times the window as the time at 1.2 GHz, and let all of PE's work inside that time shrink by half, not only the blocks one has looked at: here 41.6 less half of 23.6 is 29.8, and the cheaper slot sum and unit 15's diagonals, which have left the stage, take off an estimated 2 more. So about 28, where after has 30.65 with 3.5 us of the stage still at 1.2 GHz. Stalls close to each other can compound, so undoing one may show less than its share. A reduction that needs another engine's result goes behind the next independent work, and the work queued on that other engine ahead of the result is moved too: here either move alone left a wait of 3 to 4 us. Before a difference of 1 or 2 us in a unit is explained, compare two traces of the same code.

## What the runs showed of the hardware

- A POOL memset does not hold every DVE operation. The one-input operations from SBUF to SBUF with 750 or 6 elements per partition wait for its end: 6.92 us [rows 8], 8.71 and 3.26 us above. Those with one element per partition (0.15), a two-input operation of 128x384 (0.55), a reduction (0.54) and PSUM sources are not held. The Trainium skill, GPSIMD Engine Reference, Specifications, has contention both for 2-port modes and for two SBUF inputs; beside a memset the rows show the first half alone. The Trainium skill, VectorE: DVE Perf Modes, What auto-detection actually checks, has a 2-port mode for a single source with source and destination in SBUF and outermost non-unit dimensions both even or equal, and the held forms fit that. That these operations run in such a mode is its reading; the trace does not name modes.
- Beside POOL operations that read tensors, two-input DVE operations are held too, to the end of the POOL operation. The weights of the diagonal start at 106.31 and end at 107.74, with POOL's product from 106.11 to 107.71:

```profile
106.31 1.43 DVE L1384 TENSOR_TENSOR at<-at,sm 125x12 f32<-125x12 f32 x1
...
106.11 1.60 POOL L590 TENSOR_TENSOR pool_a<-k,pool_a 128x748 f16<-128x748 f32 x1
```

- The DVE operation that starts first is not held: the weights started 0.06 to 0.07 us ahead of a POOL cast in seven units (138.17 is one) and took their 0.17 in each.
- ACT's fills of zeros from a column, 0.86 ns per column, hold nobody: beside them DVE's scaling of 128x6 took 0.17 us (at 325.54), which memsets stretched to 0.96, 2.42 and 3.26, and its scan 1.78 as in unit 8.
